# Weighting the expert rows where they leave PSUM, and combining them by transfers that add

## What is computed

```python
x = x + gnn(layernorm(x), edges, edge_type, ...)      # 40000 edges, 8 relations, a gate
t = layernorm(x)
logits = t @ Wr.T + br                                # 8 experts
top_v, top_i = top_k(logits, 2); w = softmax(top_v)   # two experts per token
o_e = relu(t @ W1[e].T + b1[e]) @ W2[e].T + b2[e]     # 1024 -> 512 -> 1024
y = t + sum over the two experts e of w_e * o_e
out = x + layernorm(y) * gamma + beta
```

## Time and profile before

| | us |
|---|---|
| median of 3 runs (2309.03 to 2311.81) | 2311.53 |
| the profiled execution, its own time | 2309.76 |
| its span | 2308.0 |
| from the last store of expert rows to the end of the span (2204.6 to 2308.0) | 103.4 |
| TensorE (PE) busy | 2059.9 (89%) |
| VectorE (DVE) busy | 1338.3 (58%) |
| GpSimd (POOL) busy | 914.9 (40%) |
| ScalarE (ACT) busy | 818.4 (35%) |
| queues: hardware (SP) and software (POOL) | 313.16 MB, 195.65 MB |

### The profile page before, as it was taken

The page is one execution under the profiler, slowest core; times in us unless marked ns, Lnnn a source line. Parts: engine busy times, 40 slices in busy tenths (PEclk is TensorE's granted clock), DMA queues, the critical chain, the costliest instruction groups (busy, mean ns, idle before and its releaser), DMA issues. The chain is left out here.

```text
span 2308.0 us, 27801 instructions
## 1 busy us (share of the span) xinstructions
PE 2059.9 (89%) x9485; PEld 1610.2 (70%) x9485; DVE 1338.3 (58%) x2373; ACT 818.4 (35%) x1068; POOL 914.9 (40%) x805
## 2 busy tenths in 40 slices
PE   6999988899999999989999999899899199999910
PEld 5777767678888888867677677676588177888800
DVE  7578576742222222149999988889798522222158
ACT  3111121123222222235655666666444033333311
POOL 0000055546555554047777777677100111000034
PEclk9999999999999999999999999999999599999955
DMA  5222366667777777678988889884465779774163
GB/s 173 97 77 82 113 221 218 196 241 249 249 252 260 259 251 251 231 257 300 317 284 285 315 305 317 291 308 159 120 193 158 320 209 342 290 300 190 43 247 121
DMA packets 159197, 524.55 MB, mean 227 GB/s; under 512 B 33578, under 2 KB 33962, under 8 KB 157024
## 3 DMA queue, kind: packets, MB, share of 16 engines
q1 hardware_dynamic: 84752, 313.16, 38.1%
q0 software_dynamic: 70432, 195.65, 26.1%
q10 hardware_dynamic: 3888, 14.16, 1.5%
HBM read 403.66 MB, written 148.94 MB: 239 GB/s over the span
## 5 line engine op out<-in xcount | busy, mean ns | idle before, releaser
L195 PE MATMUL psum<-w_hi,xnT_hi 128*128 128x512 f32 (+1 forms) x1600 | 433.0, 406 | 12.9 <-PEq L400 6.4
L195 PE MATMUL psum<-w_lo,xnT_hi 128*128 128x512 f32 (+1 forms) x1600 | 425.3, 396 | 0.0
L195 PE MATMUL psum<-w_hi,xnT_lo 128*128 128x512 f32 (+1 forms) x1600 | 415.0, 393 | 0.0
L791 POOL DMA_INDIRECT sorted_rows<-acc x313 | 334.7, 1069 | 116.4 <-issue 85.8
L195 PEld LDWEIGHTS psum<-w_hi,xnT_hi 128*128 128x128 f32 (+1 forms) x1600 | 299.9, 191 | 84.4 <-issue 9.8
L195 PEld LDWEIGHTS psum<-w_lo,xnT_hi 128*128 128x128 f32 (+1 forms) x1600 | 299.7, 187 | 74.5
L195 PEld LDWEIGHTS psum<-w_hi,xnT_lo 128*128 128x128 f32 (+1 forms) x1600 | 296.9, 186 | 73.5
L760 DVE TENSOR_TENSOR acc<-acc 128x1024 fp32r<-128x1024 f32 x64 | 78.8, 1231 | 374.0 <-DMA split_experts<-acc 220.1
L521 ACT ACTIVATE work<-psum 128x512 f32<-128x512 f32 (+1 forms) x150 | 89.8, 599 | 546.9 <-PE psum L195 480.2
L883 POOL DMA_INDIRECT w_lo<-y_rows,sort_row x176 | 230.8, 1311 | 94.5 <-issue 57.8
L883 POOL DMA_INDIRECT w_hi<-y_rows,sort_row x176 | 235.0, 1335 | 61.9 <-issue 53.2
(11 more groups left out here) (278 smaller groups left out, 2643.5 us busy)
## 6 DMA issues: line engine op xcount, KB each, us to landing
split_experts<-acc SPq DMA_DIRECT2D x128, 512.0 KB
ring<-split_experts SPq DMA_DIRECT2D x16, 4096.0 KB, 15.1
w_raw<-in_wchunks SPq DMA_DIRECT2D x88, 512.0 KB
y_rows<-work SPq DMA_DIRECT2D x144, 256.0 KB
acc<-in_wchunks SPq DMA_DIRECT2D x64, 512.0 KB
o_rows<-o_s ACTq DMA_DIRECT2D x27, 512.0 KB
work<-local_rows SPq DMA_DIRECT2D x26, 384.0 KB
acc<-in_bias SPq DMA_DIRECT2D x10, 512.0 KB, 5.0
```

The source lines that it names most:

```text
L195: i = pe.matmul(to[:rm, :], x_[:, k, m * P:m * P + rm], w_[:, s, k * HALF:(k + 1) * HALF], start=(n == 0), stop=(n == 3 * KD - 1))
L791: pool.indirect_dma_start(sorted_dram, IndirectOffsetOnAxis(ap=e_dest[:, c:c + 1], axis=0), e_rec[:, c, :], None, bounds_check=BLOCKS * P ...
```

## The change

In the routing stage:

- `hot_low`, `hot_token` and a new `hot_weight` lie in the second half of `ring` and are float32 of the reduced kind (fp32r) instead of float16. `LISTS` = 28 columns take the place of 27.
- VectorE splits the softmax weights in a rounded part and its rest, and makes `hot_weight` (128 x 20 x 2 x 28) from them; TensorE makes 20 more products, 128x56 each; the two halves of the result are summed to `slot_w`, the weight of every place of the list.
- `token_at` is made as soon as the token list is there, ahead of the rest of VectorE's work, and GpSimd issues the first two gathers of tokens in this stage.
- SP loads only the first two halves of weights here. Halves 2 and 3 are loaded in the expert stage, after both gathers have landed, each after the half before it.

In the expert stage ScalarE's two copies to `o_s` scale by `slot_w`, and `beta` is added to `out` itself, where the gate stage now stores x1. The final stage is gone with its barrier; its work is at the end of the expert stage: GpSimd waits for the last store of expert rows, issues 20 gathers that add into `acc` (all ten tiles for the first expert, then for the second, each of these after the first has landed in its tile), and at the end ten transfers that add `acc` to `out` in DRAM. VectorE makes the statistics of a group of tiles (3, 3, 2, 2) and then their reciprocal roots together.

```diff
@@ gate stage
-                sp.dma_start(x1_dram[at, :], x_s[:rows(m), m % 2, :]).then_inc(x1_stored[m % 2], 16)
+                sp.dma_start(out[at, :], x_s[:rows(m), m % 2, :]).then_inc(x1_stored[m % 2], 16)
@@ routing stage
+        def gather_tokens(pool, b):
+            pool.indirect_dma_start(t_s[:, b % 2, :], None, t_dram, IndirectOffsetOnAxis(ap=token_at[:, b:b + 1], axis=0),
+                                    bounds_check=N - 1, oob_is_err=False).then_inc(t_in[b % 2], 16)
-            hot_low = ssb("hot_low", [P, COLS, P], F16)
+            later = ring[:, 1, :, :, :].rearrange("p a b n -> p (a b n)")
+            hot_low = later[:, 0:COLS * P].rearrange("p (c n) -> p c n", c=COLS)
                 pool.memset(t_s[:, :, :], 0.0).then_inc(made, 1)
+                pool.wait_ge(made, 7)
+                pool.wait_ge(token_ready, 1)
+                for b in range(2):
+                    gather_tokens(pool, b)
             def _(sp):
-                for n in range(RING):
+                for n in range(2):
                     load_half(sp, n, n * P)
                 i.then_inc(list_done, 1)
+                pe.wait_ge(weight_hot, 1)
+                for c in range(COLS):
+                    rm = rows(c % TILES)
+                    i = pe.matmul(bank[3][:, 0:2 * LISTS], hot_low[:rm, c, :],
+                                  hot_weight[:rm, c, :, :].rearrange("p h n -> p (h n)"), start=(c == 0), stop=(c == COLS - 1))
+                i.then_inc(weight_done, 1)
                 i.then_inc(hot_ready, 1)
+                link(v.tensor_copy(part_w[:, 0, :], weight_of[:, :, :].rearrange("p k t -> p (k t)")))
+                link(v.tensor_tensor(part_w[:, 1, :], weight_of[:, :, :].rearrange("p k t -> p (k t)"),
+                                     part_w[:, 0, :].bitcast(F32), ALU.subtract))
+                for h in range(2):
+                    i = v.tensor_tensor(hot_weight[:, :, h, :], hot_high[:, :, :],
+                                        part_w[:, h, :].bitcast(F32).unsqueeze(2).to_broadcast([P, COLS, LISTS]), ALU.mult)
+                i.then_inc(weight_hot, 1)
+                v.wait_ge(list_done, 1)
+                ... (three instructions, then)
+                v.tensor_copy(token_at[:, :], tokens[:, :]).then_inc(token_ready, 1)
                 ... (the 30 or so instructions that were there)
+                v.wait_ge(weight_done, 1)
+                link(v.tensor_copy(slot_w[:, :], bank[3][:, 0:TILES_T]))
+                link(v.tensor_tensor(slot_w[:, :], slot_w[:, :], bank[3][:, LISTS:LISTS + TILES_T], ALU.add))
@@ expert stage
                 for n in range(HALVES_E):
+                    if n == 2:
+                        for i in range(2):
+                            sp.wait_ge(t_in[i], 16)
+                    if 2 <= n < RING:
+                        load_half(sp, n, n * P)
...
                 pool.wait_ge(x1_shifted, 16 * TILES)
+                pool.wait_ge(rb_added, 2 * TILES)
+                pool.wait_ge(o_stored, 16 * BLOCKS_T)
+                for k in range(2):
+                    for m in range(TILES):
+                        if k == 1:
+                            pool.wait_ge(o_got[m], GOT[m] + 16)
+                        c = k * TILES + m
+                        pool.indirect_dma_start(acc[:rows(m), m, :], None, o_dram,
+                                                IndirectOffsetOnAxis(ap=place_i[:rows(m), c:c + 1], axis=0),
+                                                compute_op=ALU.add).then_inc(o_got[m], 16)
+                for m in range(TILES):
+                    pool.wait_ge(scaled, m + 1)
+                    pool.dma_start(out[m * P:m * P + rows(m), :], acc[:rows(m), m, :], accum_op=ALU.add).then_inc(stored, 16)
+                pool.wait_ge(stored, 16 * TILES)
...
-                    act.activation(o_s[:, 0:HALF], bank[0], ACT.Copy).then_inc(o_read, 1)
+                    act.activation(o_s[:, 0:HALF], bank[0], ACT.Copy, scale=slot_w[:, b:b + 1]).then_inc(o_read, 1)
...
+                for g, (lo, hi) in enumerate(TAIL_GROUPS):          # VectorE; TAIL_GROUPS = (0,3) (3,6) (6,8) (8,10)
+                    for m in range(lo, hi):
+                        rm = rows(m)
+                        v.wait_ge(o_got[m], GOT[m] + 32)
+                        for q in range(2):
+                            i = v.bn_stats(stats[:rm, m % 2, q, :], acc[:rm, m, q * HALF:(q + 1) * HALF])
+                        link(i)
+                        link(v.bn_aggr(aggr_of[:rm, m, :], stats[:rm, m % 2, :, :]))
+                    v.tensor_scalar(s, aggr_of[:, lo:hi, 1], EPS, None, ALU.add).then_inc(var_ready, 1)
+                    for m in range(lo, hi):
+                        v.scalar_tensor_tensor(out=o, in0=o, scalar=aggr_of[:rows(m), m, 0:1], in1=gamma_bc[:rows(m), :],
+                                               op0=ALU.subtract, op1=ALU.mult).then_inc(centred, 1)
+                    v.wait_ge(std_ready, g + 1)
+                    ... (four small instructions on [128, hi - lo], then)
+                    v.tensor_tensor(rstd_of[:, lo:hi], w, r, ALU.mult).then_inc(rstd_ready, 1)
```

More of the change, by code:

```diff
@@ L1339, in _ @@
                     rm = rows(c % TILES)
[L1340 removed]
+                    i = pe.matmul(bank[2][:, 0:LISTS], hot_low[:rm, c, :], hot_token[:rm, c, :],
                                   start=(c == 0), stop=(c == COLS - 1))
                 i.then_inc(list_done, 1)
+                pe.wait_ge(weight_hot, 1)
[4 more added lines that the diff above has]
+                i.then_inc(weight_done, 1)
             @block.vector
@@ L1484, in program @@
             rw_turned, rw_copied, rb_done, rb_added = ssem("e_rwt"), ssem("e_rwc"), ssem("e_rb"), ssem("e_rba")
+            aggr_of, var_of, std_of = ssb("aggr_of", [P, TILES, 2]), ssb("var_of", [P, TILES]), ssb("std_of", [P, TILES])
+            recip_of, w_of, rstd_of = ssb("recip_of", [P, TILES]), ssb("w_of", [P, TILES]), ssb("rstd_of", [P, TILES])
+            var_ready, std_ready, centred, rstd_ready, scaled, stored = (
+                ssem("f_var"), ssem("f_std"), ssem("f_cent"), ssem("f_rstd"), ssem("f_scaled"), ssem("f_stored"))
+            o_got = landed + [ssem("f_o8"), ssem("f_o9")]
+            GOT = [p + 16 * PASSES for p in PLACED] + [0, 0]
+            TAIL_GROUPS = ((0, 3), (3, 6), (6, 8), (8, 10))
             block = stage.enter_context(nc.Block())
@@ L1514, in gather @@
                         pool.wait_ge(t_free, b - 1)
-                    pool.indirect_dma_start(t_s[:, b % 2, :], None, t_dram,
-                                            IndirectOffsetOnAxis(ap=token_at[:, b:b + 1], axis=0),
-                                            bounds_check=N - 1, oob_is_err=False).then_inc(t_in[b % 2], 16)
-                gather(0)
-                gather(1)
+                    gather_tokens(pool, b)
                 for m in range(TILES):
-                    pool.dma_start(x1_dram[m * P:m * P + rows(m), :], beta[0:1, :].to_broadcast([rows(m), D]),
+                    pool.dma_start(out[m * P:m * P + rows(m), :], beta[0:1, :].to_broadcast([rows(m), D]),
                                    accum_op=ALU.add).then_inc(x1_shifted, 16)
@@ L1592, in _ @@
                 output(LAST)
-                act.wait_ge(o_stored, 16 * BLOCKS_T)
+                for g, (lo, hi) in enumerate(TAIL_GROUPS):
+                    act.wait_ge(var_ready, g + 1)
+                    act.activation(std_of[:, lo:hi], var_of[:, lo:hi], ACT.Sqrt).then_inc(std_ready, 1)
+                    act.wait_ge(rstd_ready, g + 1)
+                    for m in range(lo, hi):
+                        act.wait_ge(centred, m + 1)
+                        o = acc[:rows(m), m, :]
+                        act.activation(o, o, ACT.Copy, scale=rstd_of[:rows(m), m:m + 1]).then_inc(scaled, 1)
             @block.vector
@@ L1631, in _ @@
                     hidden_lo(b)
+                for g, (lo, hi) in enumerate(TAIL_GROUPS):
+                    for m in range(lo, hi):
[5 more added lines that the diff above has]
+                        link(v.bn_aggr(aggr_of[:rm, m, :], stats[:rm, m % 2, :, :]))
+                    s, std, r, w = var_of[:, lo:hi], std_of[:, lo:hi], recip_of[:, lo:hi], w_of[:, lo:hi]
+                    v.tensor_scalar(s, aggr_of[:, lo:hi, 1], EPS, None, ALU.add).then_inc(var_ready, 1)
+                    for m in range(lo, hi):
+                        o = acc[:rows(m), m, :]
+                        v.scalar_tensor_tensor(out=o, in0=o, scalar=aggr_of[:rows(m), m, 0:1], in1=gamma_bc[:rows(m), :],
+                                               op0=ALU.subtract, op1=ALU.mult).then_inc(centred, 1)
+                    v.wait_ge(std_ready, g + 1)
+                    link(v.reciprocal(r, std))
+                    link(v.tensor_tensor(w, r, r, ALU.mult))
+                    link(v.tensor_tensor(w, w, s, ALU.mult))
+                    link(v.tensor_scalar(w, w, -0.5, 1.5, ALU.mult, ALU.add))
```

(1 more changed line is left out.)

117 lines of the change are left out of this document (23 added, 94 removed).

## The result

The changed kernel takes 2293.56 us, the median of five runs (2289.25 to 2298.83), against 2311.53 (2309.03 to 2315.4). That is 18.0 us less; the ratio is 0.9922 (95% interval 0.9901 to 0.9942). The forecast was 2284 with a range of 2262 to 2301: faster, as forecast, by 18 us instead of 27. The profiled execution is the fastest of the five, 2289.25, with a span of 2287.3. One execution each of the kernels of experiments 5 and 6 ran for 6159.96 and 4125.41 us and is left out of their medians, ranges and ratios.

A forecast was written before the change was run, and what follows sets the result against it. TensorE bounds the expert stage, VectorE the old end, adding transfers the new one. Span 2308.0 less 11.3 (start) and 15.0 (end) is 2281.7, plus 1.8 around it 2283.5; forecast 2284 us, range 2262 to 2301.

The forecast's parts named there:

- Both holes: TensorE idle from 1835 to 1845 before the experts and from 2230 to the end, all the change can reach.
- the change of stage: Between VectorE's chain in the routing stage and TensorE's first tile of the expert stage, taken as 0.5 us.
- the sum of start and expert stage: 12.3 us gained at the start, less 1 us for traffic on the third block's gather: net 11.3 us.
- (a): At the end, queued adding transfers overlap at 1.3 to 1.9 us each like plain ones: 2255.5 us; chance 0.13.
- (b): At the end, adding gathers don't queue, each taking 4.8 to 5.0 us: 2341.5 us; chance 0.11.
- But their traffic lies on the gather of the third block ... I take 1 us for that: Early expert stage: late halves 2 and 3 delay the third block's token gather, 1 us, ends 0 and 5.
- (c): The start gives nothing: pairs cost 0.338, third and fourth blocks wait 5 us each for tokens: 2294.8; chance 0.14.
- The pairs: Routing stage: an fp32r load and its short product take 0.25 us, between 0.196 and 0.338.
- 54.7 and 29.8 us: At the end, DMA time for 19.5 gathers adding into SBUF, and for 9.8 transfers adding to out.
- the 3.05 taken for transfers that add to DRAM: At the end, DMA engine time in us for each 512 KB transfer adding to out, from 2.9 to 3.2.
- a lone transfer's 2.80: One 512 KB transfer adding into SBUF, alone in its window, took 2.80 us of all 16 engines.
- the 4.64 of a pair: One gather and one transfer adding to DRAM together took 58% of 8 us, 4.64 us.

The follow-up runs named there:

- experiment 5: The changed kernel with the one-hot operands in float16 in their own memory, the rest of the change kept: 2292.75 us, ratio 0.9922.
- experiment 6: The kernel of experiment 5 with halves 2 and 3 issued in the routing stage once the first two gathers have landed: 2302.11 us, ratio 0.9959.
- experiment 9: The changed kernel with two output buffers, the 20 gathers at the end not adding, so the sum is left out: 2260.57 us, ratio 0.9783.
- experiment 3: A second buffer for the expert rows: in the changed kernel 2277.87 us, ratio 0.9866; in the kernel before 2304.67 us, ratio 0.9972.
- experiment 1: The changed kernel's new end with the old start (float16 operands, all halves loaded early, first gathers in the expert stage): 2296.8 us, ratio 0.9937.
- 7: The kernel of experiment 6 with the three small b2 loads on ScalarE's queue instead of SP's: 2292.78 us, ratio 0.9896.
- 8: The kernel of 7 with two output buffers for the expert rows: 2285.64 us, ratio 0.9872.
- 11: The kernel of 8 with each tile's first gather adding into acc, its second plain and added by VectorE: 2268.35 us, ratio 0.9794.

## Why the prediction was right, and where it was not

**Right: what the change reaches.** Both holes shrank by the mechanisms named. The gather met a free queue, so that TensorE's first transposes waited for the change of stage alone, and the end is bound by adding transfers: DMA full, VectorE idle for half of it. Not right is the sum of start and expert stage, forecast as 11.3 us and 1.6 in the profiles; the end's gain, larger than forecast, made up for a part. Rivals (a) and (b) are excluded by 2.7 us of engine time for each transfer and by experiment 9. The scale in ScalarE's copies costs nothing (experiment 3).

**The step that failed: "But their traffic lies on the gather of the third block ... I take 1 us for that".** The price of that gather was right: TensorE's only wait for `t_s` in the stage was 1.30 us. What the step left out is a second party to the same traffic, the stores of the expert rows, of which only one can be under way since `o_s` is one tile. The prediction took the rest of the expert stage as unchanged. It lost 8.8 us in the profile, 366.8 against 358.0. The runs show the mechanism from both sides: with a second buffer the stage is 353.9 under the same traffic, and with `beta` moved away 358.6. The size is less certain than the cause: the kernels with the early start, halves 2 and 3 in the expert stage, `beta` in its old place and one buffer had stages of 366.8, 363.6 and 360.8 in single profiles (the last with the old end), against 358.0 and 360.8 with all halves early. Rival (c) had named late halves that take back the start, with another victim: it put them on the token gathers, which waited 1.3 us. Its 2294.8 is the number nearest to the measured 2293.56, which lies just above the forecast's own range of 2273 to 2292; of its signs only that 1.3 us appeared, and the forecast had no sign that would have shown the stores. The rows to see it were at hand. ScalarE waited 50.0 us for these stores already before, and the stage then was longer by 4 us than with two buffers.

**Start: 10.4 instead of 12.3 us.** 0.4 of the difference lies ahead of the routing stage, which began later by that much than in the profile before. The pairs were cheaper than forecast, 0.22 us for 0.25, and VectorE's chain ended about as forecast (1834.54 for 1834.8). The forecast let TensorE wait for the first gather alone and took the change of stage at 0.5 (TensorE's first transposes came 2.7 us after the chain). By the profiles the stage doesn't change until the second gather has landed. In the kernel after that gather is issued at 1831.05 and the stage begins at 1836.91, 5.86 later; in the other six with both gathers in the routing stage and no load behind them it is 5.45 to 5.74. The kernel of experiment 6 shows the landing, since SP waits for both gathers before it issues; here GpSimd's second gather and the first instruction of the next stage, SP's issue between them, and VectorE in experiment 1, where no gather lies in the routing stage:

```profile
1826.26 1.03 POOL L1269 DMA_INDIRECT t_s<-t_rows,token_at  x1 [0.30 <-issue]
1832.78 0.95 POOL L1555 MEMSET o_s<- 128x1024 f32 x1 [5.49 <-POOLq L1281]
```

```profile
1831.57 0.80 SPq L1278 DMA_DIRECT2D ring<-split_experts  x2
```

```profile
1835.83 0.18 DVE L1488 TENSOR_TENSOR slot_w<-slot_w,psum 128x27 f32<-128x27 f32 x1
1836.95 0.07 DVE L1679 MEMSET aggr_of<- 128x20 f32 x1 [0.93 <-PEq L1281]
```

The gathers have landed 5.31 us after the issue (1826.26 to 1831.57), SP's issue ends at 1832.37, and GpSimd's first instruction of the next stage comes 0.41 later (0.40 or 0.41 in the kernels of 7, 8 and 11 too). In experiment 1, without gathers, it comes 0.49 after VectorE's last, and VectorE's own first 0.93 after; in experiment 5, with them, 1.96 and 2.40. That the end of a stage waits for GpSimd's transfers fits all of these, but experiments 1 and 5 differ in the loads of the halves too, and no run varied it alone.

**End: 19.1 instead of 14.3 us**, both from the first gather's issue to the end of the span (of the forecast 15.0, 0.7 lay ahead of that issue by the same count: 102.4 less 88.1). This is a mis-sized term: 29.3 transfers at 2.7 instead of the 2.88 that 54.7 and 29.8 us make on average. The difference is 5 us, the larger part from the 3.05 taken for transfers that add to DRAM, which moved at the same 210 GB/s as the gathers (209 from 2260 to 2270 us). That a lone transfer's 2.80 and the 4.64 of a pair held some start and finish that queued ones share is likely and not shown.

**The sum.** Against the forecast 26.3 us of span, the start lacks 1.9, the stage 8.5 (it lost 8.8, and the forecast had 1.0 less the 0.7 above), and the end has 4.8 more: 20.7, the difference of the spans. The medians differ by 18.0, since the profiled run stood 4.3 below its median after and 1.8 before. The two large misses have opposite signs, and that is luck: without that of the end the forecast would have been 14 us too low instead of 10.

## What to carry to other kernels

When transfers are moved into a stretch, list everyone who waits for a transfer there, stores of single buffers first, and read how long they wait already: a wait that is hidden for 50 us at 8.7 each shows when it grows to 12.4. A second buffer for them was worth 6 us before the change and 13 to 16 after it. And an addition made by a transfer is paid in the DMA engines' time, here nearly twice that of a plain one; where both VectorE and the DMA engines have work, share the additions between them until both are full.

## What the hardware showed that was not expected

- Adding nearly doubles the price in the queue as well as alone: 2.7 us of 16 engines per 512 KB at some 210 GB/s, against 1.4 us and up to 418 GB/s for the same gathers without it. Its issue on GpSimd is longer too, 1.53 to 1.60 us against 0.95.
- Three loads of 32 KB kept ScalarE waiting for 23.8 us behind 8 MB on their own hardware queue and for 10.4 on the other one, while the same 8 MB moved.
- 512 KB stores that take 2.6 us at the quiet end of the stage kept ScalarE waiting for up to 12.4 us beside 4 MB loads and adding transfers.
- fp32r pairs of 128x128 loads and short products go by every 0.22 us at 1.2 GHz (granted clock 0.5) though each load is listed with 0.333; float16 pairs with 27 or 28 columns go by every 0.04.
- A stage with two gathers near its end and no load behind them was left only 5.5 to 5.9 us after the second was issued, though nothing in the other engines' programs waits for it there.
